# A graph layer on one core: which queue fetches 20 of its 831 edge tiles, and what VectorE's additions wait for in the first 120

## The chip, the cores and the metric

The kernel runs on one core of a Trainium2 chip. The metric is the device time of one execution in microseconds (us), median of several runs. A core has five engines with an instruction queue each: TensorE (PE: matmuls; PEld: its weight loads), VectorE (DVE), ScalarE (ACT), GpSimd (POOL) and SyncE (SP). SP and ACT issue ordinary DMAs; POOL issues indirect ones, in which 128 row numbers in SBUF name the 128 rows that are fetched (a gather). All engines run at once and order themselves by semaphores.

## The reference

There are 6250 nodes with 128 features and 106250 edges, each with a source, a destination and one of 40 relation types; the edges are sorted by destination.

```
seg = dst * 40 + edge_type
S   = segment_sum(x[src], seg).reshape(6250, 40, 128)     # sum of sources by node and relation
cnt = segment_sum(1, seg).reshape(6250, 40)
agg = einsum('nrd,rdf->nf', S, relation_weights) + cnt @ rFeatures
h   = agg * max(degree, 1) ** -0.5
y   = x + relu(h + h @ loop_weight)
out = layernorm(y)
```

## The kernel before

**Tiles and blocks.** The edges are cut into 831 tiles of 128 (the last one, tile 830, has 10). 17 tiles make a block; there are 49 blocks, the last of 15 tiles. Tile t is number k of block i, t = 17 i + k. Because the edges are sorted, a tile's destinations lie in a window of 12 nodes.

**The work of a tile.** Its 128 source rows are fetched into SBUF. VectorE builds a 0/1 matrix `hot` of 128 edges by 480 columns (40 relations times 12 nodes; `one_hot`, L815). TensorE multiplies the rows by it (L1027, two matmuls, since each fp32 row is kept as a high and a low part) and a small matmul counts edges (L1014). ScalarE copies columns 1 to 11 of the window from PSUM into the ring of partial sums (L614); VectorE adds column 0 to it (L917), and behind that addition builds `hot` of tile t + 7. The PSUM banks are six, so TensorE can start tile n only when the addition of tile n - 6, or of one nearby, is done. The 41 relation matmuls of an earlier block (L1039), some 2.4 a tile, are spread between the tiles, and so are that block's layer norm and stores.

**Where the rows come from.** The first 85 tiles (`PLAIN`) are gathered from `x` into `raw`, 34 tiles ahead at most, and split into high and low parts by ScalarE (L590) and VectorE (L811). In parallel SP, ScalarE and VectorE stage the whole of `x`, split, into a table `x_parts` in HBM (13 pieces; SP's stores are L437). From tile 85 on POOL gathers whole split rows of 1 KB from that table (L524) into 17 buffers; the gather of tile t waits until tile t - 16 is multiplied (L523).

**Tiles by row.** For the tiles in `BY_ROW` (L72) the rows are not gathered by POOL. When the staging is done, SP reads 16 row addresses at a time into registers (L475, one TENSOR_LOAD) and for each row copies its register (`snap`, L476, a MOVE) and issues one DMA of 1 KB (L477). There are eight buffers; before the tile number j of the list, SP waits until number j - 8 is multiplied (L471). SP goes through the list in its order and does nothing else from then on. The list holds tile 8 of the blocks 7, 10, ... 46 (14 tiles), of the blocks 9, 18, 27, 36 and 45, and tile 830. The five last named are shared (`BY_BOTH`): POOL gathers their first 126, 124, 127, 112 and 64 rows (L509), SP the rest. So SP issues 14 x 128 + 87 + 10 = 1889 row DMAs, POOL 85 + 726 + 5 = 816 gathers. TensorE takes the tiles strictly in order, and waits at a tile by row for all of its rows (L1018).

**The pace of VectorE.** Each addition waits, besides for its data, for the end of POOL's work on the gather of tile t + 5 (`BEHIND`, L915 and L916; `gather_issued` counts them, and `gathers_through` turns a tile number into that count).

Of the kernel before, what the change touches and what calls it, by code (L numbers as in the profile page):

```python
# [7 lines left out]
F32 = mybir.dt.float32  # L8
# [3 lines left out]
U8 = mybir.dt.uint8  # L12
F32R = mybir.dt.float32r

P = 128
# [16 lines left out]
SEG = BLOCK + WIN  # L32
AHEAD = 7
BEHIND = 5
COLS_T = TILES + TPB
POS = 20
POS_LOAD = 4
# [30 lines left out]
FREE_W = 25  # L68
PLAIN_BLOCKS = 5
PLAIN = PLAIN_BLOCKS * TPB  # L70
POOL_PART = {9: 126, 18: 124, 27: 127, 36: 112, 45: 64}
BY_ROW = [i * TPB + TPB // 2 for i in sorted([*range(7, BLOCKS - 1, 3), *POOL_PART])] + [-(-E // P) - 1]  # L72
BY_BOTH = {i * TPB + TPB // 2: n for i, n in POOL_PART.items()}
BY_ROW_BUFS = 8
ROW_BYTES = 2 * D * 4
X_ROWS = N // P
# [43 lines left out]
def build(nc, x, src_main, src_by_tile, src_rest, dst_main, dst_rest, type_main, type_rest, r_features, relation_w, loop_w, out):  # L120
    with ExitStack() as ctx:
# [151 lines left out]
        by_row_cleared = sem("by_row_cleared")  # L273
        by_row_src_loaded = sem("by_row_src_loaded")
        by_row_ready = sem("by_row_ready")
        both_landed = {t: sem(f"both_landed{t}") for t in BY_BOTH}
        by_row_landed = [sem(f"by_row_landed{j}") for j in range(len(BY_ROW))]
        gathered = [sem(f"gathered{k}") for k in range(TPB)]
        types_ready = sem("types_ready")
# [51 lines left out]

            return min(P, E - t * P)

        def first_by_row(t):

            return BY_BOTH.get(t, 0)

        def gathers_through(t):

            return t + 1 - len([n for n in BY_ROW if n <= t and n not in BY_BOTH])  # L340

        def group_of(t):

# [71 lines left out]
        @block.sync  # L415
        def _(sp):
            sp.dma_start(src[:, 0:TPB], src_main[:, 0:TPB]).then_inc(first_src_loaded, 16)
            for t, main in ((dst, dst_main), (typ, type_main)):
                sp.dma_start(t[:, 0:FULL], main).then_inc(edges_loaded, 16)
            sp.wait_ge(padded, 1)  # L420
            for t, rest in ((dst, dst_rest), (typ, type_rest)):
                sp.dma_start(t[0:REST, FULL:FULL + 1], rest).then_inc(edges_loaded, 16)
            sp.dma_start(src[:, TPB:FULL], src_main[:, TPB:FULL]).then_inc(src_loaded, 16)
            sp.dma_start(src[0:REST, FULL:FULL + 1], src_rest).then_inc(src_loaded, 16)

            def stage_load(n):

                p, rows_each, of, _ = stage_rows(n)
                to = x_in[0:p, n % 2, 0:rows_each]
                sp.dma_start(to if rows_each > 1 else to.rearrange("p n d -> p (n d)"), of).then_inc(stage_loaded[n % 2], 16)  # L430

            def stage_store(n):

                p, rows_each, _, to = stage_rows(n)
                of = x_out[0:p, n % 2, 0:rows_each].bitcast(F32)
                sp.wait_ge(stage_low, n + 1)
                sp.dma_start(to, of.rearrange("p n c d -> p n (c d)") if rows_each > 1 else of.rearrange(  # L437
                    "p n c d -> p (n c d)")).then_inc(staged[n % 2], 16)

            for n in range(STAGED_FIRST):  # L440
                stage_load(n)
            sp.dma_start(loop[:], loop_w).then_inc(loop_loaded, 16)
            sp.dma_start(x_blk[:], x[0:P, :]).then_inc(x_blk_loaded, 16)
            sp.wait_ge(const_done, 1)
            sp.dma_start(w[0:R, R, :], r_features).then_inc(w_loaded, 16)
            sp.wait_ge(by_row_cleared, 1)
            for j, t in enumerate(BY_ROW):
                of = src_by_tile[t:t + 1, :] if t < FULL else src_rest.rearrange("p o -> o p")
                sp.dma_start(by_row_src[j:j + 1, 0:rows_in_tile(t)], of).then_inc(by_row_src_loaded, 16)
            sp.wait_ge(pos_done, 1)  # L450
            sp.dma_start(pos[:].rearrange("o (b k) -> o b k", k=POS)[:, :, 0:TPB], pos_2d[:, 0:TPB]).then_inc(pos_ready, 16)
            w_v = relation_w.rearrange("r d f -> d r f")
            for r in range(FREE_W, R, W_LOAD):
                sp.dma_start(w[:, r:r + W_LOAD, :], w_v[:, r:r + W_LOAD]).then_inc(w_loaded, 16)
            sp.wait_ge(pos_ready, 16)
            for r in range(0, FREE_W, W_LOAD):
                sp.dma_start(w[:, r:r + W_LOAD, :], w_v[:, r:r + W_LOAD]).then_inc(w_loaded, 16)
            sp.wait_ge(src_loaded, 2 * 16)

            def in_order():  # L460
                for n in range(STAGES):
                    stage_store(n)
                    if n + 2 < STAGES:
                        stage_load(n + 2)
                for h in range(2):
                    sp.wait_ge(staged[h], len(range(h, STAGES, 2)) * 16)
                index = [sp.alloc_register(f"sp_row{n}") for n in range(ROW_LOAD)]
                sp.wait_ge(by_row_ready, 1)
                for j, t in enumerate(BY_ROW):
                    if j >= BY_ROW_BUFS:  # L470
                        sp.wait_ge(tile_done, BY_ROW[j - BY_ROW_BUFS] + 1)  # L471
                    for n, p in enumerate(range(first_by_row(t), rows_in_tile(t))):
                        if n % ROW_LOAD == 0:
                            m = min(ROW_LOAD, rows_in_tile(t) - p)
                            sp.load(index[0:m], by_row_at[j:j + 1, p:p + m])  # L475
                        at = sp.snap(index[n % ROW_LOAD])  # L476
                        sp.dma_start(by_row[p:p + 1, j % BY_ROW_BUFS].rearrange("p c d -> p (c d)").bitcast(U8),  # L477
                                     x_bytes[:, bass.ds(at, ROW_BYTES)]).then_inc(by_row_landed[j], 16)

            def g_load(t):  # L480
                if not isinstance(t, int):
                    sp.wait_ge(g_step, t * G_STEPS + G_SETUP)
                sp.dma_start(g_src[:], src[:, column(t)]).then_inc(g_idx, 16)

            path(sp, in_order, lambda: g_tiles(g_load)(sp))

        @block.gpsimd
        def _(pool):
# [13 lines left out]


            def gather(t):
                if t in BY_BOTH:
                    j, n = BY_ROW.index(t), BY_BOTH[t]
                    if j >= BY_ROW_BUFS:
                        pool.wait_ge(tile_done, BY_ROW[j - BY_ROW_BUFS] + 1)
                    pool.indirect_dma_start(  # L509
                        by_row[0:n, j % BY_ROW_BUFS].rearrange("p c d -> p (c d)").bitcast(F32), None, x_parts,  # L510
                        bass.IndirectOffsetOnAxis(ap=src[0:n, t:t + 1], axis=0), engine_sem=gather_issued).then_inc(
                            both_landed[t], 16)
                    return
                if t in BY_ROW:
                    return
                k = t % TPB
                at_least(pool, gathered[k], gathers_into(k, t - 1) * 16)
                n = rows_in_tile(t)
                if t >= PLAIN:
                    if t == PLAIN:  # L520
                        for h in range(2):
                            pool.wait_ge(staged[h], len(range(h, STAGES, 2)) * 16)
                    pool.wait_ge(tile_done, t - TPB + 1)  # L523
                    pool.indirect_dma_start(  # L524
                        rows[0:n, k].rearrange("p c d -> p (c d)").bitcast(F32), None, x_parts,
                        bass.IndirectOffsetOnAxis(ap=src[0:n, t:t + 1], axis=0), engine_sem=gather_issued).then_inc(
                            gathered[k], 16)
                    return
                if t >= RAW:
                    pool.wait_ge(low_done, group_of(t - RAW) + 1)  # L530
                pool.indirect_dma_start(  # L531
                    raw[:, t % RAW], None, x, bass.IndirectOffsetOnAxis(ap=src[:, t:t + 1], axis=0),
                    engine_sem=gather_issued).then_inc(gathered[k], 16)
# [195 lines left out]
        def _(dve):  # L729
# [159 lines left out]
            def step(i, tiles, sums, late, fin):  # L889
                c = i - 3  # L890
                for k in range(TPB):
                    if sums and known(i, 2) and k == SAFE:
                        merge(i, tiles)
                    if tiles and k < tiles_of(i):
# [17 lines left out]
                        if k == 0 and known(i, 1):  # L912
                            dve.wait_ge(cleared, i)
                        a = ring[:, :, bass.ds(start, 1)]
                        last = min(t + BEHIND, USED - 1)  # L915
                        dve.wait_ge(gather_issued, gathers_through(last))  # L916
                        nc.vector.tensor_tensor(a, a, win_ps[bank_of(t)][:, :, 0:1], ALU.add).then_inc(added, 1)  # L917
                        if known_less(t + AHEAD, USED):
# [70 lines left out]
        def _(pe):  # L989
# [12 lines left out]
            def tile(i, k):  # L1002
# [12 lines left out]
                                         hot_node[:, n % TPB], start=True, stop=True)  # L1015
                if not known_less(i, PLAIN_BLOCKS) or not isinstance(i, int):
                    if t in BY_ROW:
                        pe.wait_ge(by_row_landed[BY_ROW.index(t)], (rows_in_tile(t) - first_by_row(t)) * 16)  # L1018
                        if t in BY_BOTH:
                            pe.wait_ge(both_landed[t], 16)  # L1020
                    else:
                        pe.wait_ge(gathered[k], gathers_into(k, t) * 16)
                elif k % 2 == 0:
                    pe.wait_ge(low_done, i * GROUPS + k // 2 + 1)
# [160 lines left out]
```

## Time and profile before

| | us |
|---|---|
| median of 3 runs | 1070.66 (1067.93 to 1071.32) |
| the profiled execution | 1068.4 |
| its span, first to last instruction | 1066.5 |
| PE busy | 954.6 (90%) |
| POOL busy | 789.6 (74%) |
| DVE busy | 742.8 (70%) |
| ACT busy | 532.0 (50%) |
| mean granted clock of TensorE | 0.985 of full |

Busy time leaves out what a queue does to issue a DMA, so SP, which only issues, has no line in it, and the 0.30 us between two gathers of POOL is not in its 74%. A chain of waits follows the end of the program back from the last instruction, at each step to what released it.

### The profile page before, as it was taken

How to read it: one execution, taken by the hardware profiler on the slowest of the kernel's cores; microseconds unless marked ns; L12 is line 12 of the kernel's file. 1: busy time of each engine (PE TensorE's matmuls, PEld its weight loads, DVE VectorE, ACT ScalarE, POOL GpSimd, SP SyncE). 2: the span in 40 equal slices, each digit the busy share in tenths (PEclk: the TensorE clock that was granted, in tenths of full speed). 3: DMA queues.
4: the chain of work that ended last, by engine and by line, in shares of the span. 5: the costliest groups of instructions: out<-in, count | busy, mean ns of one | idle time of the engine just before them, and what ended most of it. 6: DMA issues, size and time to landing. Idle time of an engine off the chain costs nothing.

```text
span 1066.5 us, 31214 instructions
## 1 busy us (share of the span) xinstructions
PE 954.6 (90%) x6713; PEld 856.4 (80%) x6713; DVE 742.8 (70%) x2590; ACT 532.0 (50%) x1137; POOL 789.6 (74%) x831
## 2 busy tenths in 40 slices
PE   2589999899998989999998899999999899999997
PEld 1369898788888888888887798888888788888887
DVE  6698777676766776667677577767676676767663
ACT  1577555445454545555454355445545554444551
POOL 7777777777777777777777777777777777777770
PEclk9799999999999999999999899999999999999999
DMA  5852234434344443444434344343443344343330
GB/s 166 291 194 56 82 111 116 118 113 115 115 117 113 116 118 112 113 115 118 114 114 115 104 115 114 113 118 112 116 117 114 112 117 118 112 117 112 112 111 23
DMA packets 66376, 125.34 MB, mean 118 GB/s; under 512 B 18074, under 2 KB 37996, under 8 KB 66184
## 3 DMA queue, kind: packets, MB, share of 16 engines
q0 software_dynamic: 38384, 101.36, 33.5%
q1 hardware_dynamic: 13768, 15.61, 4.6%
q10 hardware_dynamic: 14032, 6.35, 2.1%
q8 instruction: 56, 0.92, 0.4%
q14 instruction: 136, 1.11, 0.3%
HBM read 113.63 MB, written 9.60 MB: 116 GB/s over the span
## 4 chain that ended last, share of the span: by engine, by line
PE 42%; DMA 25%; POOL 17%; issue 10%; ACT 1%; DVE 1%; POOLq 0%; SPq 0%; ACTq 0%; DVEq 0%
DMA rows<-x_parts,src 23%; PE win_ps L1027 21%; PE agg_ps L1039 18%; POOL rows L524 16%; PE win_ps L1112 1%; DMA x_in<-x 1%; PE win_ps L1065 1%; POOL raw L531 1%; PE win_ps L1014 1%; DMA x_out<-x_parts,src 0%; ACT ring L614 0%; POOLq L523 0%; PE win_ps L1064 0%; DMA raw<-x,src 0%; DVE ring L917 0%
## 5 line engine op out<-in xcount | busy, mean ns | idle before, releaser
L524 POOL DMA_INDIRECT rows<-x_parts,src x726 | 691.0, 952 | 221.3 <-issue 161.6
L614 ACT COPY ring<-win_ps 128x451 f32 x831 | 465.3, 560 | 371.0 <-PE win_ps L1027 230.7
L1027 PE MATMUL win_ps<-hot,rows 128*128 128x480 f32 x1622 | 557.9, 430 | 62.2 <-DMA rows<-x_parts,src 54.0
L1039 PEld LDWEIGHTS agg_ps<-ring,w 128*128 128x128 f32 x3936 | 554.9, 192 | 41.5
L1039 PE MATMUL agg_ps<-ring,w 128*128 128x128 f32 x3936 | 562.6, 275 | 0.0
L815 DVE TENSOR_SCALAR hot<-iota,key_f 128x480 fp32r<-128x480 f16 x831 | 395.2, 476 | 0.8 <-issue 0.8
L917 DVE TENSOR_TENSOR ring<-ring,win_ps 128x41 f32 x831 | 188.0, 226 | 289.4 <-DMA rows<-x_parts,src 216.7
L1027 PEld LDWEIGHTS win_ps<-hot,rows 128*128 128x128 f32 x1622 | 251.5, 193 | 101.2 <-DMA rows<-x_parts,src 91.1
L531 POOL DMA_INDIRECT raw<-x,src x85 | 90.1, 1060 | 26.0 <-issue 20.1
L1014 PEld LDWEIGHTS win_ps<-hot_node,hot_type 128*128 128x128 bf16 x831 | 80.2, 100 | 34.3 <-issue 16.1
L1014 PE MATMUL win_ps<-hot_node,hot_type 128*128 128x12 bf16 x831 | 85.6, 170 | 22.0 <-DVE ring L917 13.6
L827 DVE TENSOR_TENSOR hot_type<-iota,typ_f 128x320 bf16<-128x320 f16 x98 | 49.8, 508 | 0.0
L646 ACT ACTIVATE var_root<-var_eps 128x1 f32<-128x1 f32 x46 | 9.3, 203 | 58.0 <-DVE var_eps L859 57.9
L638 ACT ACTIVATE deg_root<-deg 128x1 f32<-128x1 f32 x46 | 9.3, 203 | 47.1 <-DVE deg L838 46.8
L875 DVE TENSOR_TENSOR ring<-ring 128x492 f32<-128x492 f32 x48 | 31.9, 665 | 0.0
L887 DVE COPY ring<-zeros 128x492 f32<-128x492 f32 x48 | 31.4, 655 | 0.0
L886 DVE COPY ring<-zeros 128x492 f32<-128x492 f32 x48 | 31.1, 647 | 0.0
L824 DVE TENSOR_TENSOR hot_node<-iota,rel_f 128x96 bf16<-128x96 f16 x98 | 25.1, 256 | 0.4 <-issue 0.4
L1065 PE MATMUL win_ps<-loop,agg_sb 128*128 128x128 f32 x96 | 22.4, 316 | 0.0
L590 ACT CAST rows<-raw 128x256 fp32r<-128x256 f32 (+1 forms) x45 | 17.4, 394 | 8.1 <-DMA raw<-x,src 8.0
L583 ACT CAST x_out<-x_in 128x512 fp32r<-128x512 f32 (+1 forms) x13 | 7.6, 595 | 27.1 <-DMA x_in<-x 13.8
L1027 PE MATMUL win_ps<-hot,x_out 128*128 128x480 f32 x40 | 14.1, 434 | 7.3 <-DMA x_out<-x_parts,src 7.3
(90 smaller groups left out, 281.2 us busy)
## 6 DMA issues: line engine op xcount, KB each, us to landing
x_out<-x_parts SPq DMA_DIRECT2D x1889, 1.0 KB
rows<-x_parts,src POOLq DMA_INDIRECT x726
x_parts<-x_out SPq DMA_DIRECT2D x12, 512.0 KB, 3.2
x_in<-x SPq DMA_DIRECT2D x12, 256.0 KB, 5.2
out<-out_sb ACTq DMA_DIRECT2D x48, 64.0 KB
x_blk<-x ACTq DMA_DIRECT2D x47, 64.0 KB
w<-relation_w SPq DMA_DIRECT2D x8, 320.0 KB
raw<-x,src POOLq DMA_INDIRECT x85
```

The source lines that it names most:

```text
L524: pool.indirect_dma_start(rows[0:n, k].rearrange("p c d -> p (c d)").bitcast(F32), None, x_parts, bass.IndirectOffsetOnAxis(ap=src[0:n, t: ...
L531: pool.indirect_dma_start(raw[:, t % RAW], None, x, bass.IndirectOffsetOnAxis(ap=src[:, t:t + 1], axis=0), engine_sem=gather_issued).then_ ...
L614: nc.scalar.copy(ring[:, :, bass.ds(start + 1, WIN - 1)], win_ps[bank_of(t)][:, :, 1:WIN]).then_inc(copied, 1)
L815: nc.vector.tensor_scalar(hot[:, buffer], iota[:], key_f[:, column(t)], None, ALU.is_equal).then_inc(hot_ready, 1)
L827: nc.vector.tensor_tensor(hot_type[:, at, 0:R], iota[:, 0:R].unsqueeze(1).to_broadcast([P, n, R]), typ_f[:, ts].unsqueeze(2).to_broadcast( ...
L875: nc.vector.tensor_tensor(ring[:, :, bass.ds(head, WIN)], ring[:, :, bass.ds(head, WIN)], ring[:, :, bass.ds(tail + BLOCK, WIN)], ALU.add) ...
L887: nc.vector.tensor_copy(ring[:, :, bass.ds(old + BLOCK, WIN)], zeros[:]).then_inc(cleared, 1)
L917: nc.vector.tensor_tensor(a, a, win_ps[bank_of(t)][:, :, 0:1], ALU.add).then_inc(added, 1)
L1014: nc.tensor.matmul(banks[bank_of(n)][:, R * WIN:COLS * WIN], hot_type[:, n % TPB], hot_node[:, n % TPB], start=True, stop=True)
L1027: ins = nc.tensor.matmul(banks[bank_of(t)][:, 0:R * WIN], of[:, part], hot[:, t % HOTS], start=False, stop=(part == PARTS - 1), skip_group ...
L1039: ins = nc.tensor.matmul(sums_of(c), w[:, r, :], ring[:, r, bass.ds(seg, BLOCK)], start=(r == 0), stop=(r == COLS - 1))
L1065: nc.tensor.matmul(ps[:, 0:D], agg_sb[:], loop[:], start=True, stop=True).then_inc(fin_done, 1)
```

## The change

Three things change.

1. `BY_ROW` becomes 19 tiles, number 8 of the blocks 7 + 40 j // 18 for j from 0 to 18 (7, 9, 11, 13, 15, 18, 20, 22, 24, 27, 29, 31, 33, 35, 38, 40, 42, 44, 47), and tile 830. All are fetched whole by SP: 19 x 128 + 10 = 2442 row DMAs. The shared tiles and their gathers on POOL go; POOL issues 811 gathers.
2. In SP's loop the 16 registers are allocated anew for each group, and `snap` takes the register over (`donate=True`) in place of copying it.
3. The addition of tile t waits for the end of the gather of tile t + max(5, 20 - t // 8): 20 tiles ahead at first, one less every 8 tiles, 5 again from tile 120 on.

```diff
+LEAD, LEAD_STEP = 20, 8
-POOL_PART = {9: 126, 18: 124, 27: 127, 36: 112, 45: 64}
-BY_ROW = [i * TPB + TPB // 2 for i in sorted([*range(7, BLOCKS - 1, 3), *POOL_PART])] + [-(-E // P) - 1]
-BY_BOTH = {i * TPB + TPB // 2: n for i, n in POOL_PART.items()}
+BY_ROW = [(7 + j * 40 // 18) * TPB + TPB // 2 for j in range(19)] + [-(-E // P) - 1]
...
-            return t + 1 - len([n for n in BY_ROW if n <= t and n not in BY_BOTH])
+            return t + 1 - len([n for n in BY_ROW if n <= t])
...
-                index = [sp.alloc_register(f"sp_row{n}") for n in range(ROW_LOAD)]
                 sp.wait_ge(by_row_ready, 1)
                 for j, t in enumerate(BY_ROW):
                     if j >= BY_ROW_BUFS:
                         sp.wait_ge(tile_done, BY_ROW[j - BY_ROW_BUFS] + 1)
-                    for n, p in enumerate(range(first_by_row(t), rows_in_tile(t))):
-                        if n % ROW_LOAD == 0:
-                            m = min(ROW_LOAD, rows_in_tile(t) - p)
-                            sp.load(index[0:m], by_row_at[j:j + 1, p:p + m])
-                        at = sp.snap(index[n % ROW_LOAD])
-                        sp.dma_start(by_row[p:p + 1, j % BY_ROW_BUFS].rearrange("p c d -> p (c d)").bitcast(U8),
-                                     x_bytes[:, bass.ds(at, ROW_BYTES)]).then_inc(by_row_landed[j], 16)
+                    for first in range(0, rows_in_tile(t), ROW_LOAD):
+                        ps = range(first, min(first + ROW_LOAD, rows_in_tile(t)))
+                        index = [sp.alloc_register(f"sp_row{j}_{p}") for p in ps]
+                        sp.load(index, by_row_at[j:j + 1, ps[0]:ps[-1] + 1])
+                        for p, reg in zip(ps, index):
+                            at = sp.snap(reg, donate=True)
+                            sp.dma_start(by_row[p:p + 1, j % BY_ROW_BUFS].rearrange("p c d -> p (c d)").bitcast(U8),
+                                         x_bytes[:, bass.ds(at, ROW_BYTES)]).then_inc(by_row_landed[j], 16)
+                        for reg in index:
+                            sp.free_register(reg)
...
-                if t in BY_BOTH:
-                    j, n = BY_ROW.index(t), BY_BOTH[t]
-                    if j >= BY_ROW_BUFS:
-                        pool.wait_ge(tile_done, BY_ROW[j - BY_ROW_BUFS] + 1)
-                    pool.indirect_dma_start(
-                        by_row[0:n, j % BY_ROW_BUFS].rearrange("p c d -> p (c d)").bitcast(F32), None, x_parts,
-                        bass.IndirectOffsetOnAxis(ap=src[0:n, t:t + 1], axis=0), engine_sem=gather_issued).then_inc(
-                            both_landed[t], 16)
-                    return
...
-                        last = min(t + BEHIND, USED - 1)
+                        last = min(t + max(BEHIND, LEAD - t // LEAD_STEP), USED - 1)
...
-                        pe.wait_ge(by_row_landed[BY_ROW.index(t)], (rows_in_tile(t) - first_by_row(t)) * 16)
-                        if t in BY_BOTH:
-                            pe.wait_ge(both_landed[t], 16)
+                        pe.wait_ge(by_row_landed[BY_ROW.index(t)], rows_in_tile(t) * 16)
```

## Rows read from the trace of the kernel before

**Rows 1.** The page: span, busy time, and the chain that ended last by engine.
```profile
span 1066.5 us, 31214 instructions
PE 954.6 (90%) x6713; PEld 856.4 (80%) x6713; DVE 742.8 (70%) x2590; ACT 532.0 (50%) x1137; POOL 789.6 (74%) x831
PE 42%; DMA 25%; POOL 17%; issue 10%; ACT 1%; DVE 1%; POOLq 0%; SPq 0%; ACTq 0%; DVEq 0%
```

**Rows 2.** POOL's timeline from 584 us: start, duration, operation, idle before it.
```profile
587.11 0.95 POOL L524 DMA_INDIRECT rows<-x_parts,src  x1 [0.30 <-issue]
588.36 0.95 POOL L524 DMA_INDIRECT rows<-x_parts,src  x1 [0.30 <-issue]
589.62 0.94 POOL L524 DMA_INDIRECT rows<-x_parts,src  x1 [0.30 <-issue]
590.86 2.55 POOL L509 DMA_INDIRECT x_out<-x_parts,src  x1 [0.30 <-PE win_ps L1027]
593.72 0.96 POOL L524 DMA_INDIRECT rows<-x_parts,src  x1 [0.31 <-PE win_ps L1027]
```

**Rows 3.** Waits: engine and line, released by; total us, times, longest.
```profile
DVE ring L917 <- DMA rows<-x_parts,src: 216.7, 402, 1.8
PEld win_ps L1027 <- DMA rows<-x_parts,src: 91.1, 169, 2.0
```

**Rows 4.** SP's TENSOR_LOADs from 199 to 261 us: duration min/median/max, first and last start.
```profile
L475 SPq TENSOR_LOAD <-by_row_at x9: 1225/1231/1293, 199.5 to 260.4; - x9
```

**Rows 5.** SP's row DMAs and MOVEs, whole span; durations ns, first and last start.
```profile
L477 SPq MOVE x_out<-x_parts x1889: 29/29/39, 76.8 to 978.2; - x189
L477 SPq DMA_DIRECT2D x_out<-x_parts x1889: 224/225/732, 76.9 to 978.2; - x189
L476 SPq MOVE  x1889: 34/34/48, 76.8 to 978.1; - x189
L449 SPq DMA_DIRECT2D by_row_src<-src_by_tile x19: 246/252/253, 6.3 to 11.6; - x19
```

**Rows 6.** One group of 16 rows in SP's timeline: start of first, us to end.
```profile
84.91 6.03 SPq L477 DMA_DIRECT2D x_out<-x_parts  x16
```

**Rows 7.** TensorE's timeline: where it takes the first, a late and the last tile by row.
```profile
176.78 0.68 PE L1027 MATMUL win_ps<-hot,x_out 128*128 128x480 f32 x2
...
993.15 0.68 PE L1027 MATMUL win_ps<-hot,x_out 128*128 128x480 f32 x2
...
1042.54 0.69 PE L1027 MATMUL win_ps<-hot,x_out 128*128 128x480 f32 x2
```

**Rows 8.** TensorE's count matmuls (one a tile) where gathers don't hold it.
```profile
80.00:110.00 30.00, 2.89 (x28) 2.77 (x28) 1.00 0.21 56
610.00:640.00 30.00, 2.82 (x28) 2.60 (x27) 1.00 0.40 112
```

**Rows 9.** TensorE's timeline around 600 us, with a wait for a shared tile.
```profile
601.32 1.14 PE L1027 MATMUL win_ps<-hot,x_out 128*128 128x480 f32 x2 [5.21 <-DMA x_out<-x_parts,src]
602.26 1.48 PE L1039 MATMUL agg_ps<-ring,w 128*128 128x128 f32 x6
603.39 1.15 PE L1027 MATMUL win_ps<-hot,rows 128*128 128x480 f32 x2
...
605.28 1.15 PE L1027 MATMUL win_ps<-hot,rows 128*128 128x480 f32 x2
...
607.28 0.68 PE L1027 MATMUL win_ps<-hot,rows 128*128 128x480 f32 x2
```

**Rows 10.** POOL's busy time in gathers of the first 142 us, by stretch (L531, then L524).
```profile
27.00:39.00 12.00, 9.26 (x10) 0.78 0.96 312
39.00:59.00 20.00, 15.74 (x15) 0.70 0.83 275
59.00:118.00 59.00, 45.58 (x45) 0.97 0.33 97
...
118.00:142.00 24.00, 18.30 (x17) 1.00 0.36 101
```

**Rows 11.** VectorE's additions (L917), count by stretch.
```profile
27.00:59.00 32.00, 4.92 (x22) 0.73 0.88 289
59.00:80.00 21.00, 4.14 (x20) 1.00 0.53 171
80.00:110.00 30.00, 6.26 (x28) 1.00 0.21 56
110.00:120.00 10.00, 1.37 (x6) 0.83 0.23 60
120.00:142.00 22.00, 4.98 (x22) 1.00 0.37 105
```

**Rows 12.** Lines of the page: all gathers of shared tiles; a small SP DMA to landing.
```profile
L509 POOL DMA_INDIRECT x_out<-x_parts,src x5 | 6.7, 1333 | 1.5 <-issue 1.2 <-PE win_ps L1027 0.3
src<-src_main SPq DMA_DIRECT2D x1, 8.5 KB, 1.8
```

## What the change should do to the time

> **What bounds the kernel now.** I read the page's busy times and chain first, then POOL's timeline, the waits, and last SP's queue, which the page's busy table leaves out. TensorE is busy 90% of the span, yet the chain is 42% TensorE and 42% gathers (DMA 25%, POOL 17%) [rows 1]: something else sets the pace and TensorE follows. POOL's timeline shows it: a gather is 0.95 us and the next starts 0.30 us later, whatever goes on elsewhere, one per 1.25 us [rows 2]. VectorE's additions end their idle time with gathers 402 times, TensorE's weight loads 169 times [rows 3]. TensorE alone would need 30 us for 28 tiles, 1.07 each [rows 8]. So from some 142 us on POOL sets the pace, with 0.18 us a tile of slack on TensorE, and a tile that POOL need not gather saves its 1.25 us. The second thing to see is SP. Its 1889 row DMAs run from 76.9 to 978.2 us without a break [rows 5], and TensorE takes the last whole tile at 993.15 [rows 7]. SP is nearly full already; before asking what POOL gains, the change must be costed there.
>
> **SP's new list.** A whole tile costs SP the time between the first load of one and of the next: 199.5 to 260.4 us, eight loads and 128 rows, 60.9 us [rows 4], or 0.476 us a row. Of this 16 rows take 6.03 us from first to last end [rows 6], 0.387 a row from start to start ((6.03 - 0.225) / 15), and the load of 1.23 us in every 16 is the rest. The 0.387 hold three records: a MOVE of L476 (34 ns), a MOVE of L477 (29) and the DMA (225) [rows 5], 288 ns busy and some 99 of gaps. The donated register removes the MOVE of L476. The one of L477 comes with the DMA of a run-time address and stays, and so do DMA and load. What goes with it: at least its own 34 ns, at most 34 and all gaps, 133. The nearest row for an issue without run-time address is that of L449, 19 in 11.6 - 6.3 us, 0.294 each [rows 5], a saving of 0.093. I take 0.060: its 34 ns and a somewhat smaller share than a third of the gaps, since the long DMA keeps more. A tile then costs 60.9 - 128 x 0.060 = 53.2 us; the ends are 56.5 (34 ns) and 43.9 (133 ns), with 49.0 by the static issue.
>
> SP starts its rows at 76.9 as before: it waits for the staging, whose last VectorE part comes before the addition of tile 31, and that addition's new wait (gather 48) is about when the old kernel reached it. So whole tile n (1 to 19) is issued by 76.9 - 1.3 + 53.2 n (the first load lies ahead of 76.9) and landed 1.8 us later by a small SP transfer [rows 12]: tile n at 77.4 + 53.2 n.
>
> **When TensorE wants them.** In the old trace the first is taken at 176.8 and that of block 46 at 993.2 [rows 7], 39 blocks, 20.9 us a block. The new tiles are 2.22 blocks apart, 37.8 tiles of which POOL gathers 36.8: 46 us at 1.25. SP delivers one per 53.2. The first lands at 130.6, 46 us early; 7.2 of the lead goes with each tile, and it is used up after 6 to 7. From there TensorE waits at each tile by row, some 7 us. The eight buffers do not help: they let SP run ahead, and SP is behind. Nothing else makes up for it. TensorE takes tiles in order, VectorE and ScalarE follow it, and POOL's gathers stop 16 tiles ahead of the tile that stands. Between two waits TensorE needs 37.8 x 1.07 = 40.4 us, and after 5.2 us of waiting the trace shows its clock low: matmul pairs of 1.14 to 1.15 us until some 606 against 0.68 from 607.28, three tiles in 5.96 us instead of 3.2 [rows 9], 2.8 lost. 43 is still under 53, so SP's pace holds to the end.
>
> **The end.** The 19th whole tile is tile 807: 77.4 + 19 x 53.2 = 1088.2. From there to tile 830 are 23 tiles at 1.07, 24.6, and the 2.8 of the low clock: 1115.6. The gathers of the next 16 are in by then, the last seven come at 1.25 behind and arrive in time; SP's last ten rows take 5 us and hide. From tile 830 the old trace takes 1066.5 - 1042.5 = 24.0 to its end [rows 1, 7], relation matmuls and layer norm that the change leaves. The span: 1139.6. The profiled run was 1.9 over its span (1068.4), and the median 2.3 over that: 1139.6 + 4.2 = 1143.8 us.
>
> **POOL's part** is then hidden: five gathers less, 8.2 us of POOL with their idle time (6.7 + 1.5) [rows 12]. It pays only in the rival below. One of them, of 127 rows, took 2.55 us [rows 2] and TensorE waited 5.21 us for its tile [rows 9]. (The Trainium skill, page DMA: Bandwidth & Descriptors, section Why a DMA increments its semaphore by 16 and not by 1, says that a transfer runs on the largest number of DMA engines up to 16 that divides its slowest dimension, so on one for 127. The trace agrees: 2.55 us beside 0.95. Whole tiles avoid it, which is a reason for the change.)
>
> The same page speaks against my forecast. In its section Issuing engines are not separate DMA queues it says that where a DMA is issued saves only the sequencer's time, usually small beside the transfer; by that SP's issue would hide and the result be that of the first rival. The rows of SP's queue differ here: 60.9 us of issue for 128 KB.
>
> **The additions' wait.** VectorE's wait blocks everything queued behind it: `hot` of tile t + 7, the low parts, the layer norm; TensorE waits for those. The price is bounded by how far ahead of the new line the old kernel was. The line asks 8 tiles per 7 gathers, 1.09 us a tile. The old additions run at 28 in 30 us from 80 to 110 and 22 in 22 from 120 [rows 11]: a little faster, so the wait does hold them back, by up to some 6 us at a time, and it is back at 5 tiles by tile 120, when the old kernel is there too. What it can bring is undisturbed gathers: 10 from 27 us took 9.26, but 15, 45 and 17 from 39, 59 and 118 took 15.74, 45.58 and 18.30 [rows 10] where 0.945 each would be 14.2, 42.5 and 16.1, an excess of 1.6 + 3.1 + 2.2 = 6.9 us while VectorE ran free of POOL. Only the last two can go, since the line is reached about tile 22. Between nothing and 5.3 I take 3. In the forecast SP ends the chain, and it is worth nothing; if it delayed tiles 0 to 120 by 6 us that would also be hidden, under a lead of SP of 46.
>
> **Rivals.** First, the other side: **SP keeps up and POOL sets the pace.** It decides where a whole tile costs so little that the 19th lands before TensorE wants it, at 993.2 + 17 x 1.25 - 11 = 1003 (tile 807 is 17 behind tile 790): 77.4 + 19 T under 1003 gives T below 48.7, a saving of 0.095 us a row. Then five gathers (8.2) and the quiet start (3) go: 1066.5 - 11.2 = 1055.3, a median of 1059.5 (1057 to 1062.5 by the bounds of the wait). For it: the static issue comes within 0.002 of that saving, a register just written might cost the DMA behind it time that no row separates, and spacing and lead are even. Against it: one MOVE of 34 ns must take 61 ns of gaps with it.
>
> Second, **the change of registers does nothing**: the copy stays, or something takes its time. SP then needs 60.9 a tile, the 19th lands at 77.4 + 1157 = 1234.5, and the end is 51.4 + 4.2 later, 1290. The MOVE of L476 stands on the very line of the copy that `donate` avoids, so this is unlikely.
>
> Third, **in between**: a tile between 48.7 and 51 us, SP late by little, 1060 to 1102.
>
> **How the numbers follow.** The forecast, a tile of 51 to 56.5 us, has 0.50; SP keeping up 0.33; in between 0.10; nothing saved 0.07. The range takes in the first three as far as a tile of 54.5 us (53.2 + 1.3, times 19 is 25 more): 1054 to 1169. By itself the likeliest case has 1102 to 1169, and up to 1206 with 34 ns. About 0.3%, 3 us, is what a measurement of this kernel can tell from no change. Faster by more: 0.33. Within: 0.03. Slower: 0.64, the forecast, the second rival and most of the third.
>
> **What would show it.** Right: L476 has no record; the loads of L475 from one tile to the next are 53 us apart; TensorE's waits for x_out grow from the sixth or seventh tile by row on, and the chain names SP's row DMAs; SP's last row is near 1091. Wrong: row DMAs of L477 end before 1000 (first rival), a tile of 61 us (second). For the start: POOL's gathers from 59 to 142 us at 0.95 and not 1.02, and additions ended by gathers from tile 22 on. What would make it wrong above all is the price of the MOVE: each 10 ns a row is 1.28 us a tile and 24 us at the end.

## The result and the profile after

The changed kernel takes 1128.08 us (median of 5 runs, 1127.53 to 1128.99), the one before 1070.66 us; the ratio is 1.054, 95% interval 1.0526 to 1.0555. It is slower, as forecast, and 16 us faster than the 1144 forecast.

The page of the changed kernel, first the span and busy times, then the chain that ended last, by engine and by line (the line numbers moved: L471 is the row DMA, L468 the load of 16 addresses, L1012 the window matmul, L1024 the relation matmul):

```profile
span 1125.7 us, 30453 instructions
PE 943.4 (84%) x6713; PEld 862.4 (77%) x6713; DVE 737.0 (65%) x2590; ACT 531.8 (47%) x1137; POOL 797.8 (71%) x826
SPq 61%; PE 18%; issue 13%; DMA 1%; DVE 0%; ACT 0%; ACTq 0%; DVEq 0%
SPq L471 47%; SPq L468 14%; PE agg_ps L1024 9%; PE win_ps L1012 8%; PE win_ps L1097 1%; DMA x_out<-x_parts 0%; DMA x_parts<-x_out 0%; PE win_ps L1050 0%; PE win_ps L1001 0%; PE win_ps L1049 0%; PE win_ps L1101 0%; DVE h_sb L833 0%; DVE y_sb L837 0%; DVE y_mid L843 0%; DVE y_sum L840 0%
```

Against [rows 1] the chain has changed owner: SP's queue was 0% of it and is 61%, the gathers were 42% and are gone. Every engine is busy for a smaller share of the span than before. That is how a bound in a queue looks: nothing in the busy times names it. POOL's busy time in us even rose, from 789.6 to 797.8, although it issues five gathers fewer: from 142 to 480 us its gathers from `x_parts` take 0.95 us as before, and from 480 us on, just before TensorE's first wait for rows, 0.99 us (418 gathers; 0.95 in the kernel before). POOL is off the chain there, so this costs nothing.

SP's instructions in the changed kernel: the loads from 756 to 810 us, and the row DMAs of the whole span, with who waited for them:

```profile
L468 SPq TENSOR_LOAD <-by_row_at x9: 1241/1257/1420, 755.6 to 808.0; - x9
...
L471 SPq MOVE x_out<-x_parts x2442: 29/29/43, 76.0 to 1074.7; - x188
L471 SPq DMA_DIRECT2D x_out<-x_parts x2442: 224/225/337, 76.1 to 1074.7; - x188
...
  PE win_ps L1012: 113.3, 9
```

Eight loads and 128 rows take 808.0 - 755.6 = 52.4 us, against 60.9 in [rows 4]. Of the three records of a row in [rows 5] two are left, as long as before, and the MOVE of the copy has none. SP's last row is issued at 1074.7 instead of 978.2, without a break, and TensorE now waits for rows, 113.3 us in 9 waits, 12.6 us each. Where, its timeline shows (start, duration, and in brackets the wait before it; six of the 19 whole tiles, and tile 830 last):

```profile
494.50 1.17 PE L1012 MATMUL win_ps<-hot,x_out 128*128 128x480 f32 x2 [8.11 <-DMA x_out<-x_parts]
...
546.99 1.17 PE L1012 MATMUL win_ps<-hot,x_out 128*128 128x480 f32 x2 [14.61 <-DMA x_out<-x_parts]
...
652.19 1.17 PE L1012 MATMUL win_ps<-hot,x_out 128*128 128x480 f32 x2 [11.56 <-DMA x_out<-x_parts]
...
866.31 0.68 PE L1012 MATMUL win_ps<-hot,x_out 128*128 128x480 f32 x2
...
1019.13 1.17 PE L1012 MATMUL win_ps<-hot,x_out 128*128 128x480 f32 x2 [13.41 <-DMA x_out<-x_parts]
...
1075.53 0.68 PE L1012 MATMUL win_ps<-hot,x_out 128*128 128x480 f32 x2
...
1101.93 0.69 PE L1012 MATMUL win_ps<-hot,x_out 128*128 128x480 f32 x2
```

The first wait is at the eighth whole tile, block 22. The waits come at tiles 2 blocks after the last one; at those 3 blocks after it (866.31 is block 38, 1075.53 block 47) there is none, and TensorE runs at its high clock there: the matmul pair takes 0.68 us, and 1.17 after each wait. The granted clock of three stretches behind the last wait says the same:

```profile
1019.00:1022.00 3.00, 2.87 (x10) 2.66 (x11) 0.00 (x0) 0.00 (x0) 0.00 (x0) 0.50 0.03 8
1022.00:1025.00 3.00, 3.00 (x20) 2.75 (x20) 1.51 (x6) 1.28 (x3) 1.53 (x2) 0.81 0.08 15
1025.00:1028.00 3.00, 3.00 (x26) 2.80 (x25) 2.15 (x9) 2.55 (x6) 2.29 (x3) 1.00 0.51 142
```

The third number from the right is the granted clock: 0.50 of full, which is 1.2 of 2.4 GHz, and 1.00 from 1025 on.

### The profile page after: what moved, and what is told of

Read it like the earlier page. It is cut to its first block, busy times and chain, and to the rows that moved or that the text cites. A ratio compares the mean times of both kernels' runs of the same rounds, so it can differ in the third digit from the quotient of the medians.

```text
span 1125.7 us, 30453 instructions
## 1 busy us (share of the span) xinstructions
PE 943.4 (84%) x6713; PEld 862.4 (77%) x6713; DVE 737.0 (65%) x2590; ACT 531.8 (47%) x1137; POOL 797.8 (71%) x826
## 4 chain that ended last, share of the span: by engine, by line
SPq 61%; PE 18%; issue 13%; DMA 1%; DVE 0%; ACT 0%; ACTq 0%; DVEq 0%
SPq L471 47%; SPq L468 14%; PE agg_ps L1024 9%; PE win_ps L1012 8%; PE win_ps L1097 1%; DMA x_out<-x_parts 0%; DMA x_parts<-x_out 0%; PE win_ps L1050 0%; PE win_ps L1001 0%; PE win_ps L1049 0%; PE win_ps L1101 0%; DVE h_sb L833 0%; DVE y_sb L837 0%; DVE y_mid L843 0%; DVE y_sum L840 0%
## 5 line engine op out<-in xcount | busy, mean ns | idle before, releaser
L511 POOL DMA_INDIRECT rows<-x_parts,src x726 | 707.5, 975 | 271.6 <-issue 184.1
L1024 PEld LDWEIGHTS agg_ps<-ring,w 128*128 128x128 f32 x3936 | 563.0, 194 | 42.7
L1012 PE MATMUL win_ps<-hot,rows 128*128 128x480 f32 x1622 | 554.9, 430 | 27.7 <-DMA rows<-x_parts,src 22.9
L1024 PE MATMUL agg_ps<-ring,w 128*128 128x128 f32 x3936 | 569.5, 278 | 0.0
L1012 PEld LDWEIGHTS win_ps<-hot,rows 128*128 128x128 f32 x1622 | 256.2, 196 | 45.0 <-DMA rows<-x_parts,src 35.7
L1012 PE MATMUL win_ps<-hot,x_out 128*128 128x480 f32 x40 | 18.0, 540 | 113.3 <-DMA x_out<-x_parts 113.3
L1012 PEld LDWEIGHTS win_ps<-hot,x_out 128*128 128x128 f32 x40 | 7.8, 243 | 114.1 <-DMA x_out<-x_parts 114.1
L1049 PEld LDWEIGHTS win_ps<-ones,cnt_sb 128*128 128x128 f32 x96 | 17.9, 188 | 3.2 <-ACT agg_sb L620 0.5
```

The lines of the kernel that those rows point to most:

```text
L511: pool.indirect_dma_start(rows[0:n, k].rearrange("p c d -> p (c d)").bitcast(F32), None, x_parts, bass.IndirectOffsetOnAxis(ap=src[0:n, t: ...
L1012: ins = nc.tensor.matmul(banks[bank_of(t)][:, 0:R * WIN], of[:, part], hot[:, t % HOTS], start=False, stop=(part == PARTS - 1), skip_group ...
L1024: ins = nc.tensor.matmul(sums_of(c), w[:, r, :], ring[:, r, bass.ds(seg, BLOCK)], start=(r == 0), stop=(r == COLS - 1))
```

## Experiments

The theory under test: the time of the changed kernel is the time that SP needs to issue its rows, and nothing else of the change costs anything. The rivals: TensorE's low clock, the number of tiles by row as such, or the additions' wait.

**The copy back in** (one word of the changed kernel):

```diff
-                            at = sp.snap(reg, donate=True)
+                            at = sp.snap(reg)
```

> The changed kernel with one word undone: SP copies each row's register again instead of taking it over. Theory (SP's issue sets the time): a row costs 0.384 us again instead of 0.318, a whole tile 60.9 instead of 52.4 us, the 19th whole tile is issued 19 x 8.45 = 160 us later, at 1231, and the time is 1128 + 160 = 1288 us, with the three waits of TensorE for tiles by row growing on nearly all of them. Rival (the row DMAs are slow in the DMA engines, or TensorE's low clock sets the time): within 1% of 1128.

Measured: 1292.74 us (two executions, 1288.18 and 1297.31), ratio to the kernel before 1.210 (1.2057 to 1.214). SP's loads and TensorE's waits in that kernel:

```profile
L468 SPq TENSOR_LOAD <-by_row_at x9: 1241/1247/1258, 744.3 to 805.2; - x9
...
L471 SPq DMA_DIRECT2D x_out<-x_parts x2442: 224/225/315, 75.7 to 1237.7; - x188
...
PE win_ps L1012 <- DMA x_out<-x_parts: 288.6, 17, 23.2
```

A tile costs 805.2 - 744.3 = 60.9 us again, SP's last row is issued 163 us later (1237.7 against 1074.7), and the time rises by 165. TensorE waits at 17 tiles instead of 9. A MOVE of 34 ns, 2442 times, off every computing engine, is worth 165 us: the theory holds and the rival of within 1% falls.

**17 tiles instead of 19:**

```diff
-BY_ROW = [(7 + j * 40 // 18) * TPB + TPB // 2 for j in range(19)] + [-(-E // P) - 1]
+BY_ROW = [(7 + j * 40 // 16) * TPB + TPB // 2 for j in range(17)] + [-(-E // P) - 1]
```

> The changed kernel with 17 whole tiles by row, 2.5 blocks apart (every 42.5 tiles), instead of 19. Theory: TensorE asks for one every 41.5 x 1.25 = 51.9 us and SP delivers one per 52.4 with a lead of 46, so no wait for a tile by row; POOL sets the pace with 814 gathers, two ordinary ones in place of five shared ones of 8.2 us: 8.2 - 2.5 = 5.7 less, and 3 less from the early wait: a span near 1058 and a time of 1060 us, ratio 0.990. Rival (the wait of the additions or the register code costs the time): above 1100.

Measured: 1059.89 us, ratio 0.9921 (0.9907 to 0.9934), faster than both kernels. Span, chain, and SP's rows in that kernel:

```profile
span 1058.2 us, 29927 instructions
...
PE 37%; DMA 27%; POOL 17%; issue 11%; DVE 1%; POOLq 0%; DVEq 0%; ACT 0%
...
L471 SPq DMA_DIRECT2D x_out<-x_parts x2186: 224/225/328, 75.5 to 969.5; - x199
L468 SPq TENSOR_LOAD <-by_row_at x137: 1132/1251/1422, 74.2 to 965.4; - x137
...
1006.41 0.68 PE L1012 MATMUL win_ps<-hot,x_out 128*128 128x480 f32 x2
```

The chain is that of [rows 1] again, SP is not in it, TensorE waits for no tile by row, and it takes the last whole tile at 1006.4, whose rows SP had issued by 965.4 (the start of the load for tile 830). Register code, additions' wait and whole tiles are all in this kernel; two tiles less for SP are the difference between 0.992 and 1.054. The gain of 0.8% is clear of its interval, but small. The number of tiles by row changes here together with SP's time; the run with the copy, with the same 19 tiles, separates the two.

**The additions' wait alone**, in the kernel before:

```diff
-                        last = min(t + BEHIND, USED - 1)
+                        last = min(t + max(BEHIND, 20 - t // 8), USED - 1)
```

> The kernel before with the early wait of the additions alone. Theory: POOL's gathers from 59 to 142 us lose 5.3 us to VectorE running free; held in step they lose about 2, the kernel is 3 us faster, 1067.5, ratio 0.997 (0 to 5.3 us, 0.995 to 1.000). Rival: the wait delays TensorE in blocks 1 to 6 and the delay stays, 3 to 6 us slower, ratio 1.003 to 1.006.

Measured: 1065.38 us against 1068.69, ratio 0.9972 (0.9961 to 0.9983). POOL's gathers in two stretches of that kernel, columns as in [rows 10]:

```profile
59.00:118.00 59.00, 44.80 (x44) 0.97 0.31 98
...
118.00:142.00 24.00, 18.21 (x20) 1.00 0.38 108
```

From 118 us on 20 gathers, some of them cut by the ends of the stretch, take the POOL time that 17 took in [rows 10]. Before 118 the gain is small: 44 take 44.80 against 45 in 45.58, 1.02 and 1.01 us each. The last gather from `x` starts at 116.1 us there and at 117.5 in the kernel before, 1.4 earlier; the rest of the 3.3 comes after it.

**Taking the registers over alone**, in the kernel before (its list and its shared tiles stay; the loop over the rows is that of the changed kernel, from `first_by_row(t)`):

```diff
-                        at = sp.snap(index[n % ROW_LOAD])
+                            at = sp.snap(reg, donate=True)
```

> The kernel before with the registers taken over instead of copied, nothing else. Theory: SP's rows cost 0.318 us instead of 0.384 and its last row is issued near 978 - 1889 x 0.066 = 853 us instead of 978, or later where it waits for a buffer; nobody waited for SP before, so the time stays, 1070.7, ratio 1.000 within 0.002. Rival (SP held POOL or TensorE back in the kernel before): over 0.3% faster.

Measured: 1067.52 us, ratio 0.9994 (0.9984 to 1.0003), no change. SP's rows:

```profile
L477 SPq DMA_DIRECT2D x_out<-x_parts x1889: 224/225/668, 76.7 to 851.9; - x189
```

SP is done 126 us earlier than in [rows 5] and nobody profits, because nobody waited for it. The same MOVE that is worth 165 us in one kernel is worth nothing in the other.

**The eight other runs met another condition of the chip.** In them the kernel before itself took 1670 to 1705 us, beside 1069 in the four runs above, on the same chip in part (chip 4 served both). Each ratio stands against the kernel before as measured beside that run, and must not be set beside those above. What the condition is, the traces show only in part. These are SP's rows in the changed kernel without the early wait, and the head of its chain:

```profile
L471 SPq MOVE x_out<-x_parts x2442: 2/29/1388, 109.0 to 1566.0; - x188
L471 SPq DMA_DIRECT2D x_out<-x_parts x2442: 2/224/777, 109.1 to 1566.1; - x188
...
SPq 58%; issue 33%; PE 3%; DVE 0%; ACT 0%; DVEq 0%; DMA 0%; ACTq 0%
...
POOL rows L511 <- issue: 188.5, 573, 4.2
PEld win_ps L1001 <- issue: 112.6, 79, 8.6
ACT ring L601 <- issue: 87.0, 157, 14.3
```

The medians of MOVE and DMA are those of the changed kernel (29 and 224 ns), but single ones take up to 1388 ns, and 2442 rows take 1457 us, 0.597 each, against 0.409 ((1074.7 - 76.1) / 2442). The time is lost in stretches of a few us, spread over the whole run. These are all of SP's row records in one of them, 3.6 us long:

```profile
L471 SPq MOVE x_out<-x_parts x5: 15/18/700, 474.5 to 478.1; - x5
L471 SPq DMA_DIRECT2D x_out<-x_parts x4: 5/9/13, 474.5 to 478.1; - x4
```

Four rows take 3.6 us, with records of the DMA of 5 to 13 ns instead of 225: one or two instructions come every 0.7 us or so, whatever they are. In this trace 779 of SP's 5036 steps from one record to the next are 0.6 to 0.8 us long, in that of the changed kernel one is; they make up most of the 458 us that the rows take more. ACT, POOL and TensorE too have pauses with nothing in the profile to wait for, ACT up to 14.3 us at a time. SP seems to be the bound for the kernel before too: it has no trace of its own here, but in e7_shared112, where SP has 1882 rows instead of 1889, TensorE waits for SP's rows 13 times:

```profile
PE win_ps L1027 <- DMA x_out<-x_parts: 351.7, 13, 34.2
```

| run | change | rows of SP | SP's rows took, us | time, us | kernel before, us | ratio |
|---|---|---|---|---|---|---|
| e5_112rows | changed kernel, 112 rows per tile by SP | 2138 | 1342 | 1509.72 | 1669.99 | 0.904 (0.900 to 0.908) |
| e6_nolead | changed kernel without the early wait | 2442 | 1457 | 1624.81 | 1669.99 | 0.974 (0.969 to 0.979) |
| e7_shared112 | before, shared tiles 112 rows each by POOL | 1882 | 1481 | 1666.96 | 1669.99 | 0.998 (0.996 to 1.001) |
| e8_18tiles | changed kernel, 18 tiles | 2314 | 1422 | 1583.26 | 1669.99 | 0.946 (0.942 to 0.950) |
| e9_112rows_again | as e5 | 2138 | 1384 | 1548.77 | 1702.45 | 0.910 (0.905 to 0.914) |
| e10_18tiles_load32 | 18 tiles, 32 addresses a load | 2314 | 1454 | 1617.00 | 1702.45 | 0.951 (0.947 to 0.954) |
| e11_18tiles_load32_again | as e10 | 2314 | 1457 | 1613.31 | 1704.76 | 0.946 (0.943 to 0.949) |
| e12_donate_lead | before with both other parts | 1889 | 1298 | 1480.70 | 1701.02 | 0.871 (0.867 to 0.875) |

The third and fourth columns are counts and first-to-last times of SP's row DMAs in each trace. e5 and e9 are one kernel, so differences of some 3% between sets of runs (1342 and 1384, 1510 and 1549 us) mean nothing here.

112 rows, run twice (16 rows of each whole tile are left out, so this kernel computes something else):

```diff
+        def rows_by_row(t):
+            return min(112, rows_in_tile(t))
...
-                    for first in range(0, rows_in_tile(t), ROW_LOAD):
+                    for first in range(0, rows_by_row(t), ROW_LOAD):
...
-                        pe.wait_ge(by_row_landed[BY_ROW.index(t)], rows_in_tile(t) * 16)
+                        pe.wait_ge(by_row_landed[BY_ROW.index(t)], rows_by_row(t) * 16)
```

> The changed kernel in which SP fetches only the first 112 rows of each of the 19 whole tiles; the last 16 rows are left out, so those tiles are computed with stale rows. TensorE, POOL and VectorE do what they do in the changed kernel. Theory: a tile costs SP 52.4 x 7/8 = 45.9 us, TensorE asks every 46, so it waits for none; POOL sets the pace with 811 gathers: 8.2 and 3 us less than the 1066.5 of the kernel before, span 1055, time 1058 to 1060, ratio 0.989. Rival (19 tiles by row cost TensorE or the DMA engines more than SP's time): above 1080.

> The run with 112 rows by SP in each of the 19 tiles (the last 16 are left out, those tiles are computed with stale rows), once more, where the kernel before takes 1070 us. Theory: SP spends 45.9 us a tile, TensorE asks every 46 us and waits for no tile by row; with 811 gathers and the early wait the time is 2.5 us under the 1059.9 of 17 tiles, 1057 to 1060, ratio 0.990. Rival (19 tiles by row cost more than SP's time): above 1080.

Beside e6, measured against the same times of the kernel before, SP fetches 12.4% fewer rows, the time is 115 us less and SP's rows take 115 less: the time follows SP's rows one for one. What the expectations put in numbers, a kernel of 1058 us with 19 tiles, could not be measured here. (e6 also lacks the early wait.)

No early wait in the changed kernel:

```diff
-LEAD, LEAD_STEP = 20, 8
+LEAD, LEAD_STEP = 0, 8
```

> The changed kernel without the early wait of the additions (5 tiles ahead throughout). Theory: SP ends the chain, so the wait neither costs nor brings anything: 1128 within 2 us. Rival: the wait delays the start of SP's rows or TensorE's first tiles, and without it the kernel is 3 to 6 us faster; or it brings its 3 us here too, and the kernel is 3 us slower.

This does not answer its question, for want of the changed kernel itself in the same condition. It shows something else: here the list of 19 tiles with registers taken over is 2.6% faster than the kernel before, while the whole change is 5.4% slower otherwise. That is not the list's doing: with the registers taken over and the old list the ratio is 0.871 (e12_donate_lead, below; it has the early wait too, which alone brought 0.3% in the other condition), so 19 tiles cost time here too.

112 rows of each shared tile:

```diff
-POOL_PART = {9: 126, 18: 124, 27: 127, 36: 112, 45: 64}
+POOL_PART = {9: 112, 18: 112, 27: 112, 36: 112, 45: 112}
```

> The kernel before with 112 rows of each shared tile gathered by POOL instead of 126, 124, 127, 112 and 64; SP fetches 16 of each, 80 rows in place of 87. Theory: the long gather of 127 rows (2.55 us, 10.3 us to landing) and TensorE's wait of 5.2 us at its tile go, POOL saves 1.6 us there and some 1 us while TensorE catches up: ratio 0.998, at most 0.997. Rival (the long gather is a chance delay of that run): ratio 1.000 and a gather as long elsewhere.

The time is unchanged within its interval, and does not tell what the long gather costs where POOL is the bound, since here TensorE waited for SP. The gathers can still be read, first those of the kernel before with the early wait (its list has the 127 rows), then those of this one (durations min/median/max):

```profile
L509 POOL DMA_INDIRECT x_out<-x_parts,src x5: 907/990/2545, 212.1 to 966.1; - x5
```

```profile
L509 POOL DMA_INDIRECT x_out<-x_parts,src x5: 932/970/1162, 273.1 to 1507.3; - x5
```

The long gather of [rows 2] is there again in the other trace, 2545 ns, so it is no chance delay, and with 112 rows it is gone, 1162 at most.

18 tiles, and 18 tiles with 32 addresses a load, the latter run twice (the edit of `ROW_LOAD` is in those two alone):

```diff
-ROW_LOAD = 16
+ROW_LOAD = 32
...
-BY_ROW = [(7 + j * 40 // 18) * TPB + TPB // 2 for j in range(19)] + [-(-E // P) - 1]
+BY_ROW = [(7 + j * 40 // 17) * TPB + TPB // 2 for j in range(18)] + [-(-E // P) - 1]
```

> The changed kernel with 18 whole tiles by row, 2.35 blocks apart. Theory: TensorE asks for one every 39 x 1.25 = 48.8 us, SP delivers one per 52.4; the lead of 46 shrinks by 3.6 a tile and is gone after 13; the 18th is issued at 76.1 + 18 x 52.4 - 1.4 = 1018 against 1004 where POOL would have TensorE. 14 late, less what TensorE catches up after blocks 3 apart: 1067 to 1077 us, ratio 0.997 to 1.006. Rival (SP isn't what decides between 17 and 19): halfway between those two, near 1094.

> 18 whole tiles, and 32 row addresses per TENSOR_LOAD instead of 16. Theory: the load of 16 takes 1.25 us and of 2 to 4 about 0.55 to 0.72, so 0.05 us a register and one of 32 takes 2.0 instead of two of 1.25: a tile costs SP 50.4 instead of 52.4, the 18th is issued at 982, before TensorE wants it at 1005, and one gather less than with 17 tiles gives 1058.6 us, ratio 0.991. Rival (the load costs by the register only, 0.078 each): a tile stays at 52.4, the 18th is 12 us late, about 1073, ratio 1.004.

> 18 whole tiles and 32 row addresses per TENSOR_LOAD, once more, where the kernel before takes 1070 us. Theory: with a load of 32 of 2.12 us, as the last run showed, a tile costs SP 52.4 - 8 x 1.25 + 4 x 2.12 = 50.9 us; the 18th is issued at 76 + 18 x 50.9 - 2 = 990, before TensorE wants it at 1005; one gather less than with 17 tiles: 1058.6 us, ratio 0.991. Rival (SP isn't what decides, the count of tiles by row is): halfway between 17 and 19 tiles, near 1094, ratio 1.023. On a chip whose SP queue stalls between rows: ratio 0.95 as in the last run.

The number of tiles orders the times as SP's rows do (0.946 with 18, 0.974 with 19 and no early wait, against the same times of the kernel before). SP's loads in e10_18tiles_load32:

```profile
L468 SPq TENSOR_LOAD <-by_row_at x73: 6/2123/2296, 109.2 to 1561.6; - x73
```

The load of 32 addresses took 2.12 us at the median, against two of 1.25, so it costs less than by the register alone. In this condition that brings nothing that can be seen (0.951 and 0.946 against 0.946 with loads of 16); whether it lets 18 tiles beat 17 in the other one stays open, as does the time of 18 tiles itself there.

The kernel before with both other parts, its own list kept (the edits of e3_lead_alone and e4_donate_alone together):

> The kernel before with its own list (14 whole tiles and five shared ones) and both other parts of the change: registers taken over, and the early wait. Where the kernel before takes 1070 us: donate alone gave 0.9994 and the wait alone 0.9972, so 0.9966, 1065 us, if they add up. Where it takes 1670 to 1705 us because SP's queue stalls between instructions: theory (those stalls are counted in instructions of SP): a row is two records instead of three, rows cost 0.60 us as in the run without the early wait there instead of the 0.79 of the run with shared tiles of 112 rows, 1889 rows are issued 0.19 x 1889 = 360 us earlier, ratio near 0.80. Rival (the stalls hold all engines alike): ratio 0.95 or more.

Measured 0.871, between the two. SP's 1889 rows take 1298 us, 0.687 a row: less than the 0.787 of e7 with the copy, more than the 0.597 of e6. So fewer instructions of SP do bring the time down there, and the rival of 0.95 falls, but my count of the pauses per instruction falls too: with the same code a row costs 0.687 in one list and 0.597 in the other. In e6 TensorE stands more of the time (308 us in 17 waits for rows by SP), here 143 in 10. Counted in the traces, 0.155 of SP's steps are pauses of 0.6 to 0.8 us in e6, 0.158 in e7 and 0.188 in e12. The pauses may then be shared between the queues that run, but no run separates that, and it stays open.

## Why the prediction was right, point by point

**The bound.** That POOL set the pace and SP was nearly full was read from the rows before; the last two tiles of SP decide, as 17 against 19 show, and the time follows SP's rows, as the run with the copy shows (19 x 8.5 = 161 us more for SP, 165 more in all).

**The price of the row** was the term that everything hung on. Taken 0.060 us for the MOVE that goes, measured (60.9 - 52.4) / 128 = 0.066: its 34 ns and 32 ns of gaps, which is a full third of the 99 between three records. The argument that the long DMA would keep more of them was wrong. DMA, second MOVE and load stayed as said. The rest of a tile's cost came out as summed, 52.4 against 53.2.

**When TensorE starts to wait.** Forecast after 6 to 7 tiles, seen at the eighth.

**How it waits** is the step that failed. I took the mean distance of 37.8 tiles and had TensorE wait at every tile, to the last, and put each wait at some 7 us, where my own terms gave 53.2 - 43.2 = 10; the nine took 12.6 on average. The distances are 34 or 51 tiles. Over 34 TensorE needs 34 x 1.07 and the 2.8 of the forecast, 39.2 us, and waits out the rest of SP's 52.4, 13 us, as the trace has it (8 to 15 us). Over 51 it needs 1075.53 - 1019.13 = 56.4, more than SP, and arrives after the rows. The last distance is one of 51, so the last stretch was TensorE's. This is how it starts:

```profile
1021.23 1.15 PE L1012 MATMUL win_ps<-hot,rows 128*128 128x480 f32 x2
...
1023.12 0.68 PE L1012 MATMUL win_ps<-hot,rows 128*128 128x480 f32 x2
```

The tile by row and the next take 1023.12 - 1019.13 = 4.0 us at the low clock, where two at 1.07 are 2.1. The 1.9 lost and 51 x 1.07 = 54.6 are the 56.4 together. From 1019.13 on nothing but TensorE stands in the way, so these 1.9 us are in the time of the kernel; at the waits before, SP's pace hides them.

**The end, term by term.** SP's loads in the changed kernel, the last of them for tile 830:

```profile
L468 SPq TENSOR_LOAD <-by_row_at x153: 1148/1252/1458, 74.8 to 1070.5; - x153
```

The 19th whole tile is issued at 1070.5 and there by about 1071.5, and not at 1088.2: 16.7 less, of which 19 x 0.8 = 15.2 is the row and the rest the start and the landing (the 18th's rows end at 74.8 + 18 x 52.4 = 1018.0 and TensorE goes on at 1019.13, 1.1 us and not 1.8). TensorE takes it at 1075.5: 4.0 more, of which the 1.9 of the low clock are a part. From there to tile 830 26.4 and not 27.4: the 2.8 for the low clock fall away, as no wait lies before it, but the 23 tiles took 1.15 each and not 1.07, 1.8 more. Together 1.0 less. The tail is 23.8, not 24.0. Median over span 2.4, not 4.2: 1.8 less. In all 16.7 - 4.0 + 1.0 + 0.2 + 1.8 = 15.7: 1143.8 - 15.7 = 1128.1. The wrong step cost only 4 us because TensorE came just that much after the rows; that is luck. The range of 1054 to 1169 held three cases of either sign and says little; what was borne out is the likeliest case, whose own range began at 1102.

**The additions' wait** was put at 3 us (0 to 5.3) in a kernel that POOL paces. Alone it brought 3.3 (0.9972). In the changed kernel the gathers are quieter too; these are its stretches from 59 and from 118 us:

```profile
59.00:118.00 59.00, 44.55 (x45) 0.97 0.34 98
...
118.00:142.00 24.00, 18.20 (x20) 1.00 0.39 108
```

At 0.945 each the 45 would be 42.5, so 2.0 of the excess of 3.1 are still there, and of the 2.2 after 118 nothing. That this gain is hidden when SP ends the chain was argued; the run for it met the other condition, so it is not shown.

**The rival that SP keeps up** had 0.33. Its point of decision fits: at 52.4 us a tile is over the 48.7 that 19 tiles allow by its sum. 17 tiles, at which SP keeps up, gave a ratio of 0.992; two gathers of 1.25 us fewer would make it 0.990 with 19, as it had summed (1059.5 of 1070.66). 19 tiles with SP out of the way were not measured in this condition. The Trainium skill, page DMA: Bandwidth & Descriptors, section Issuing engines are not separate DMA queues, has issuing elsewhere save only sequencer time, usually small beside the transfer. By that SP's issue would hide. In the kernel before it does, 126 us of it could go without effect (e4_donate_alone); in the changed one it does not, and is 61% of the chain.

**The rival that nothing is saved** is the run with the copy: forecast 1290, measured 1292.7.

## What to carry to other kernels

A queue that only issues has no busy time, so cost it separately: instructions by start-to-start distance, up to the moment at which someone needs the last of them, and compare with the time that is there. When work moves to such a queue the margin is used up first, and then each further unit costs its full time: here 17 tiles were 0.8% faster and 19 were 5.4% slower, and 161 us more for SP on top of that cost 165. Take the real distances between deadlines, not their mean, since the last one decides who ends.

## What was not expected of the hardware

A register MOVE of 34 ns costs SP 66 ns from start to start, beside a DMA issue of 225. After a wait of 8 to 15 us a matmul pair takes 1.17 us and not 0.68, the granted clock of the span falls from 0.985 to 0.935, and yet only the last of the nine spells at the low clock cost time, 1.9 us. And the time of this kernel depends on a condition under which the queues pause, SP's row going from 0.409 to 0.597 us on average and the kernel before from 1069 to 1670 us or more; there the change without its early wait comes out 2.6% faster and not slower, because taking the registers over, worth nothing to the kernel before in the one condition, brings it with the early wait to 0.871 in the other. What sets the pauses was not found.
